# An output projection placed inside the attention's last head, earlier query rows, and wider fills of the relative terms

## The reference

```python
x = x + attention(layernorm(x, eps=1e-6))      # 12 heads of 32 channels
t = tokens(x)                                  # 2304 x 384
t = t + moe(layernorm(t, eps=1e-5))            # 8 experts, 1536 wide, top 2

# attention, per head; Rh, Rw gathered from relative position tables
attn = softmax((q * 32 ** -0.5) @ k.T + rel_h[..., :, None] + rel_w[..., None, :])
out = concat(attn @ v) @ proj_w + proj_b
```

## Time and profile before

| | |
|---|---|
| three timed runs | 2270.21 us median, 2269.88 to 2273.95 |
| profiled execution | 2271.55 us, its span 2269.8 us |
| busy in the span | PE 2056.3, PEld 1801.0, DVE 1423.4, ACT 1481.7, POOL 919.2 us |
| relative terms, DVE's first to last fill | 132.7 to 216.5 us |
| attention, last operation of DVE | 1444.9 us |
| projection, DVE's first and last operation | 1454.5 and 1523.6 us |
| gates, DVE's first operation | 1524.0 us |
| experts, POOL's first gather | 1617.1 us |

### The profile page before, as it was taken

How to read it: one execution, slowest core, us unless ns; L and a number is a source line. 1 busy time by engine, 2 the same in 40 slices (tenths; PEclk the granted TensorE clock), 3 DMA queues, 4 the chain that set the end, 5 groups by cost and what they waited for, 6 DMA issues and landing times. The chain is left out here.

```text
span 2269.8 us, 34244 instructions
## 1 busy us (share of the span) xinstructions
PE 2056.3 (91%) x11132; PEld 1801.0 (79%) x11132; DVE 1423.4 (63%) x2321; ACT 1481.7 (65%) x2533; POOL 919.2 (40%) x621
## 2 busy tenths in 40 slices
PE   6965589999999999999999999674799999999997
PEld 6932278888888888888888888462688888989997
DVE  5665679898998998989899996377333443110000
ACT  3354078888888888888888889412355555555554
POOL 0061323333333333333333334480555666555553
PEclk9955689999999999999999999787699999999999
DMA  6699933665546455563565534422433443211111
GB/s 215 220 253 271 182 84 69 117 112 104 108 73 133 87 111 94 106 131 71 110 113 107 113 66 99 129 101 73 160 85 105 140 125 99 49 37 29 29 29 15
DMA packets 92822, 247.02 MB, mean 109 GB/s; under 512 B 10168, under 2 KB 44440, under 8 KB 88420
## 3 DMA queue, kind: packets, MB, share of 16 engines
q1 hardware_dynamic: 81024, 223.57, 40.9%
q0 software_dynamic: 10672, 20.46, 5.4%
q10 hardware_dynamic: 960, 0.80, 0.1%
HBM read 179.27 MB, written 65.52 MB: 108 GB/s over the span
## 5 line engine op out<-in xcount | busy, mean ns | idle before, releaser
L896 DVE TENSOR_REDUCE mx<-ps_m 128x1 f32<-128x384 f32 x1212 | 643.7, 553 | 109.6 <-PE ps_m L751 104.3
L608 POOL TENSOR_TENSOR p_lo<-p_f,p_hi 128x768 fp32r<-128x768 f32 x216 | 398.1, 1843 | 767.8 <-ACT p_f L855 767.8
L849 ACT ACTIVATE p_hi<-ps_s 128x768 fp32r<-128x768 f32 x648 | 528.5, 816 | 147.2 <-PE ps_s L765 143.6
L855 ACT ACTIVATE p_f<-ps_s 128x768 f32<-128x768 f32 x648 | 525.7, 811 | 0.0
L751 PE MATMUL ps_m<-key_hi,query_hi 128*128 128x384 f32 x1240 | 419.4, 345 | 44.5 <-DMA query_hi<-rel_hi_d 35.7
L608 DVE TENSOR_TENSOR p_lo<-p_f,p_hi 128x768 fp32r<-128x768 f32 x432 | 414.2, 959 | 37.5 <-ACT p_f L855 36.4
L762 PE MATMUL ps_s<-query_hi,key_hi 128*128 128x384 f32 x1296 | 338.2, 342 | 10.4 <-DMA query_rest<-m_d 8.3
L775 PE MATMUL ps_o<-p_hi,val 128*65 128x384 f32 x1296 | 331.3, 337 | 1.7 <-POOL p_lo L608 1.7
L765 PE MATMUL ps_s<-query_rest,key_rest 121*128 121x384 f32 x1296 | 331.8, 337 | 0.0
L775 PE MATMUL ps_o<-p_lo,val 128*65 128x384 f32 x1296 | 331.5, 337 | 0.0
L751 PEld LDWEIGHTS ps_m<-key_hi,query_hi 128*128 128x128 f32 x1240 | 232.5, 189 | 89.0 <-DMA query_hi<-rel_hi_d 39.3
(11 more groups left out here) (247 smaller groups left out, 2242.5 us busy)
## 6 DMA issues: line engine op xcount, KB each, us to landing
query_rest<-rel_lo_d SPq DMA_DIRECT2D x36, 864.0 KB
query_rest<-qk_lo_d SPq DMA_DIRECT2D x36, 576.0 KB
query_rest<-qk_hi_d SPq DMA_DIRECT2D x36, 576.0 KB
query_hi<-rel_hi_d SPq DMA_DIRECT2D x12, 864.0 KB, 19.3
w_raw__19867<-w_u SPq DMA_DIRECT2D x12, 768.0 KB, 5.8
w_raw__19868<-w_u SPq DMA_DIRECT2D x12, 768.0 KB, 4.3
w_raw__19869<-w_u SPq DMA_DIRECT2D x12, 768.0 KB, 4.5
w_raw__19870<-w_u SPq DMA_DIRECT2D x12, 768.0 KB, 4.4
```

Source lines behind the costliest of these rows:

```text
L608: engine.tensor_tensor(p_lo[r][:], p_f[idx % 2], p_hi[r][:].bitcast(F32), ALU.subtract).then_inc(lo_done(0, idx)[0], 1)
L849: act.activation(p_hi[r][:], ps_s[:, bank:bank + 2, 0:TB], ACT.Exp).then_inc(hi_ok, 1)
L855: act.activation(p_f[idx % 2], ps_s[:, bank:bank + 2, 0:TB], ACT.Exp).then_inc(f_ok, 1)
L896: dve.tensor_reduce(mx[s // TILES][:, s // 3 % 6, col:col + 1], ps_m[:, c, 0:TB], AX.X, ALU.max).then_inc(mx_ok, 1)
```

## The change

**Projection into the last head.** `phase_proj` is gone. Its work stands in the attention stage. The heads 0 to 10 are projected for 18 tiles of 128 tokens by "all" jobs of nine matmuls; the last head is projected from ps_o's own copy by "own" jobs of three matmuls, and scaled afterwards, on the way out, by the reciprocal of its own sum, which a further column of the weights (C + 2 columns) carries along. Jobs stand on PE between the scores and `pv` of a unit, use the two halves of ps_m in turn, and are given units by two formulas: all t in unit 27 + 4t//3; own t < 6 in 29 + t, own 6 to 11 in 37 + t, own 12 to 17 after the loop. The proj_w rows are loaded at the end of head 8's list on SP (five DMAs) and split by POOL in units 11 and 14 of head 10 and by DVE in units 1 and 2 of the last head. The bias is a row of the weights against a row of ones.

The sums of heads 0 to 7 are loaded in head 10, those of 8 to 10 in the last head; DVE takes reciprocals (unit 26 of head 10; unit 12 of the last head), SP writes them and loads them back spread over 32 rows a head (`spread`, into `share`, the place of head 10's keys and queries, 8 and 3 DMAs of 288 KB). The spread of heads 0 to 7 stands in SP's list ahead of `load_max(11, 2)`. DVE multiplies in nine `scale` steps of 128x768 in units 11 to 16 and 21 to 23; POOL copies the high part of each tile, DVE subtracts for the low part two units before the job, and DVE evicts a job in the unit after it, with the bn_stats of the layernorm. x is loaded into the place of `share` as the scales free it. The last head's output is no longer stored to o_d.

**Query and key rows.** For h < 10, `load_hi(h + 2)` stands before the store of block 2 and waits for the scores of head h only.

**Wide fills.** CPB goes from 2 to 4: a fill is four matmuls in two PSUM banks (four rings of 4 x 256), 24 fills a group.

**Expert weights.** Expert 0's six pieces are no longer split in the projection. SP loads four of them at the start of the gates stage and two more ahead of the stores of blocks 2 and 3; POOL splits pieces 0 and 1 in the gates stage, DVE pieces 2 to 5 at the start of the experts stage, ahead of expert 1's.

```diff
 # phase_rel
-        CPB = 2
-        BANKS = 8
+        CPB = 4
+        RINGS = 4
+        WIDE = 256
-                        last = pe.matmul(ps[0:SIDE, bank, n * NQ:(n + 1) * NQ],
+                        last = pe.matmul(ps[0:SIDE, ring, n, 0:NQ],
...
 # phase_attention, SP
             def rest(h, par):
                 sp.wait_ge(pv_ok, UNITS * h + RING)
                 load_kv(h + 1, 1 - par)
                 for b in range(QBLOCKS):
+                    if b == QBLOCKS - 1 and h < HEADS - 2:
+                        sp.wait_ge(s_ok, UNITS * (h + 1))
+                        load_hi(h + 2, par)
                     store(h, par, b)
+                    if h == HEADS - 2 and b == 0:
+                        joins(QBLOCKS * EARLY)
+                        sp.dma_start(flat_early[:], flat(sums_d, 0, EARLY)).then_inc(sums_in, 16)
                     sp.wait_ge(s_ok, UNITS * h + TILES * (b + 1))
                     load_rest(h + 1, b)
+                    if h == HEADS - 2 and b == 0:
+                        for c in range(2):
+                            sp.dma_start(room[:, c, :], o_d[c * P:(c + 1) * P, :]).then_inc(early_in, 16)
+                    if h == HEADS - 2 and b == 1:
+                        sp.wait_ge(rec_ok, 1)
+                        sp.dma_start(flat(rec_d, 0, EARLY), flat_early[:]).then_inc(rec_out, 16)
                     if b < 2:
                         load_max(h + 1, b)
-                if h < HEADS - 2:
-                    sp.wait_ge(s_ok, UNITS * (h + 1) + LEAD)
-                    load_hi(h + 2, par)
+                if h == HEADS - 2:
+                    sp.wait_ge(s_ok, UNITS * (h + 1))
+                    sp.wait_ge(rec_out, 16)
+                    for c in range(2):
+                        spread(c, HPT)
+                    joins(QBLOCKS * (HEADS - 1))
+                    sp.dma_start(flat_late[:], flat(sums_d, EARLY, LATE)).then_inc(sums_in, 16)
+                    sp.wait_ge(raw_zero, 5)
+                    sp.dma_start(room[0:P - HD, 2, :], o_d[2 * P:C - HD, :]).then_inc(late_in, 16)
+                    sp.wait_ge(rec_ok, 2)
+                    sp.dma_start(flat(rec_d, EARLY, LATE), flat_late[:]).then_inc(rec_out, 16)
+                    sp.wait_ge(rec_out, 32)
+                    spread(2, LATE)
                 load_max(h + 1, 2)
+                if h == HEADS - 4:
+                    load_weights()
+                if h == HEADS - 2:
+                    for g in range(QBLOCKS):
+                        load_x(g)
...
 # phase_attention, PE
+            def tail(kind, t):
+                n = number_of[kind, t]
...
+                if n >= 2:
+                    pe.wait_ge(evicted, n - 1)
...
+                if kind == "all":
+                    pe.wait_ge(low_ok, t + 1)
+                    hi, lo = part_hi[t % len(part_hi)], lows[:, :, t * P:(t + 1) * P]
+                    for m, (v, w) in enumerate([(hi, w_hi), (hi, w_lo), (lo, w_hi)]):
+                        for k in range(KC):
+                            last = pe.matmul(ps_m[:, n % 2, 0:C], v[:, k, :], w[:, k, :], start=(m + k == 0), stop=(m == 2 and k == KC - 1))
+                else:
+                    b, c, cut = t // TPQ, t % TPQ // TPB, slice(t % TPB * P, (t % TPB + 1) * P)
+                    pe.wait_ge(acc_d, ACC + 2 * b + c + 1)
+                    for m, (v, w) in enumerate([(ot_hi, own_w_hi), (ot_hi, own_w_lo), (ot_lo, own_w_hi)]):
+                        last = pe.matmul(ps_m[:, n % 2, 0:C + 2], v[:, c, cut], w[:], start=(m == 0), stop=(m == 2))
+                last.then_inc(tail_mm, 1)
...
 # phase_attention, DVE
+            def scale(n):
+                c, cols = n // QBLOCKS, slice(n % QBLOCKS * QB, (n % QBLOCKS + 1) * QB)
+                rows = P if c < 2 else P - HD
+                if n == 0:
+                    dve.wait_ge(early_in, 32)
+                if n == 6:
+                    dve.wait_ge(late_in, 16)
+                if n % QBLOCKS == 0:
+                    dve.wait_ge(spread_in[c], 16 * (HPT if c < 2 else LATE))
+                dve.tensor_tensor(room[0:rows, c, cols], room[0:rows, c, cols], share[0:rows, c, cols], ALU.mult).then_inc(scaled, 1)
...
+            def added(kind, t):
+                n = number_of[kind, t]
...
+                    dve.reciprocal(rec[:, t:t + 1], ps_m[:, n % 2, C:C + 1]).then_inc(rec_made, 1)
+                    dve.wait_ge(evicted, n)
+                    dve.wait_ge(rec_made, t + 1)
+                    dve.scalar_tensor_tensor(x1[:, t, :], ps_m[:, n % 2, 0:C], rec[:, t:t + 1], x1[:, t, :], ALU.mult, ALU.add).then_inc(evicted, 1)
+                    if t > 0:
+                        measured(t - 1)
...
 # phase_gates, SP
-            for i in range(PIECES, PIECES + RAWS):
+            for i in range(RAWS):
                 moe.load_piece(sp, i)
...
+                if 2 <= blk < 2 + SPLIT_EARLY:
+                    sp.wait_ge(moe.w_ok, blk - 1)
+                    moe.load_piece(sp, RAWS + blk - 2)
                 sp.wait_ge(xn_ok, blk + 1)
```

More of the change, by code:

```diff
@@ L584, in phase_attention @@
         low_out = [sem(f"low_out{i}") for i in range(2)]
-        all_in = sem("all_in")
+        raw_zero = sem("raw_zero")
+        raw_in = sem("raw_in")
+        w_split = sem("w_split")
+        w_low = sem("w_low")
+        sums_in = sem("sums_in")
+        rec_ok = sem("rec_ok")
+        rec_out = sem("rec_out")
+        early_in = sem("early_in")
+        late_in = sem("late_in")
+        spread_in = [sem(f"spread_in{c}") for c in range(KC)]
+        scaled = sem("scaled")
+        x_in = [sem(f"x_in2_{b}") for b in range(QBLOCKS)]
+        part_ok = sem("part_ok")
+        low_ok = sem("low_ok")
+        tail_mm = sem("tail_mm")
+        evicted = sem("evicted")
+        rec_made = sem("rec_made")
         block = ctx.enter_context(nc.Block())
         loop_heads = OALL_HEADS
+        ACC = QBLOCKS * (HEADS - 1) + 1
+        TPQ = TILES // QBLOCKS
+        steps = {}
+        for t in range(TILES):
+            steps.setdefault(FIRST_TILE + 4 * t // 3, []).append(("all", t))
+            steps.setdefault((29 + t if t < TPQ else 37 + t) if t < 2 * TPQ else UNITS, []).append(("own", t))
+        order = [s for k in sorted(steps) for s in sorted(steps[k])]
+        number_of = {s: n for n, s in enumerate(order)}
+        unit_of = {s: k for k in steps for s in steps[k]}
         def chunk_at(h, par, k):
@@ L733, in head @@
                     n = QBLOCKS * h + idx // TILES - 1
-                    if idx % TILES == JOIN and idx < UNITS and n >= 0:
+                    if idx % TILES == JOIN and idx < UNITS and 0 <= n < QBLOCKS * (HEADS - 1):
                         joined(n)
+                    if h == HEADS - 2:
+                        if idx in SPLITS_AT:
+                            split_weights(SPLITS_AT.index(idx))
+                    if last:
+                        for t in range(TILES):
+                            if idx <= unit_of["all", t] - 2 < idx + POOL_EVERY:
+                                high_part(t)
             for idx in range(POOL_EVERY - 1, FIRST - 1, POOL_EVERY):
@@ L804, in head @@
                         half(tp, s, 0, ps_m)
+                    if last:
+                        for job in order:
+                            if unit_of[job] == k:
+                                tail(*job)
                     if k % TILES == 0:
-                        pe.wait_ge(acc_a, QBLOCKS * h + k // TILES + 1)
-                        pe.wait_ge(acc_d, QBLOCKS * h + k // TILES + 1)
+                        made = QBLOCKS * h + (k // TILES if not last else 2 * (k // TILES)) + 1
+                        pe.wait_ge(acc_a, made)
+                        pe.wait_ge(acc_d, made)
                     if k % TILES < TILES - 1:
@@ L813, in head @@
                         half(tp, s, 1, ps_m)
+                if last:
+                    for job in order:
+                        if unit_of[job] == UNITS:
+                            tail(*job)
             pe.wait_ge(hi_in[0], 48)
@@ L924, in head @@
                         negated(number, s)
+                    if last:
+                        for job in order:
+                            if unit_of[job] == k + 2 and job[0] == "all":
+                                low_part(job[1])
+                        for job in order:
+                            if unit_of[job] == k - 1:
+                                added(*job)
+                if last:
+                    for job in order:
+                        if unit_of[job] >= UNITS - 1:
+                            added(*job)
+                    measured(TILES - 1)
             dve.sem_inc(acc_d, 1)
@@ L1359, in _ @@
             pool.tensor_tensor(b2_lo[:], b2_raw[:], b2_hi[:].bitcast(F32), ALU.subtract).then_inc(b2_lo_ok, 1)
+            for i in range(SPLIT_EARLY):
+                moe.split_piece(pool, i)
             for t in range(TILES):
@@ L1819, in _ @@
         def _(dve):
```

(2 more changed lines are left out.)

341 lines of the change are left out of this document (149 added, 192 removed).

## The result

The changed kernel takes 2244.69 us in the median (four runs, 2238.38 to 2245.71), the kernel before 2270.05 beside it: ratio 0.9877, 95% interval [0.9857, 0.9897]. A later comparison gave 0.9886 [0.9865, 0.9906]. The profiled run took 2243.93, its span is 2242.2, 27.6 less than before.

What follows compares the result with a forecast made beforehand. PE was taken to bound the full heads, while no engine filled the projection. The terms - 5.8 - 2.0 - 25.4 + 0.5 + 2.4 = - 30.3 us took 2271.55 to 2241.2, or 2240 against the median; range 2228 to 2256.

Steps and rivals of the forecast that it cites:

- the fourth: Rival: earlier loads and wide fills give nothing, as another wait takes their place; 7.8 us less gain, 2248; chance 0.10.
- Query and key rows: Attention heads: loading these rows earlier removes PE's whole wait for them, minus 5.8 us (bounds minus 9.0 and minus 3).
- Wide fills: Attention's start: twelve wide fills save DVE 4.8 us, later restarts cost up to 2.0; taken as minus 2.0.
- in between: Among the wide fills: where the DMA engines are full, an earlier fill gives nothing; part of taking minus 2.0 us.
- The projection: Last head and after: the 79.6 us stage goes, less 34.8 matmuls, 8.5 DVE work, 10.9 after the loop: 25.4 us less.
- weight lows: Last head, units 1 and 2: DVE's low parts of the projection weights hold up its work by 1.5 us.
- the job units: Last head, units 27 to 49: 198 matmuls add 34.8 us on PE, nine units with both job kinds 2.2 more.
- rival 3: DVE and POOL block each other on SBUF operands: nine scales grow by 10.8 us, giving 2250; chance 0.12.
- Gates: Gates stage: two more loads ahead of stores, each after a POOL split ending in time; plus 0.5 us (0 to 6).
- Experts: Experts' start: expert 0's four splits on DVE slow two POOL subtractions on the filling pipeline's path; plus 2.4 us (0 to 6).
- Rival 2: Last head: spread sums arrive late, DVE waits in units 11, 12 or 21; 3 to 13 us, 2248; chance 0.12.
- Rival 1: Projection jobs: each waits for the eviction of the one just before; 40 us on top, 2280; chance 0.05.

Runs made afterwards that it cites:

- before_hi: The kernel before with only the next head's query and key rows loaded earlier, ahead of the store and of query_rest: 2261.16 us, ratio 0.9956.
- gate_late: The changed kernel with POOL's two early weight splits waiting until DVE has normalised all blocks, their reloads behind all stores of xn_d: 2243.61 us, ratio 0.9874.
- all_moved: The changed kernel with first m_d ahead of query_rest blocks 1 and 2, late POOL splits, weights' low parts in units 19 and 20, scales from unit 12: 2238.28 us.
- after_again: The changed kernel run again, nothing changed, on the chip of the follow-up runs as their base: 2246.58 us.

## Why the prediction was right

The forecast was 2240 us, the median is 2244.69; the mechanism held. Of the rivals, the half of the fourth that speaks of the wide fills came, and the third's mechanism at under a third of its price. By its terms, each from edges of the two traces (sum -27.6):

- *Query and key rows*, predicted -5.8, measured -5.2 by the maxima. That has the reciprocal in head 10 in it, which the prediction counts with the projection: over units 26 to 28 of that head PE's matmuls into ps_o fall back 0.8 us against before, as predicted. Without it the rows gave -6.0. The nearness hides two errors. The move alone is worth 8.3 (run before_hi), near the -9.0 of PE's weight loads that I kept as a bound; and the changed buffer addresses, which I put at nothing, cost 0.25 us a head, 2.3 over the heads in this count.

```profile
1307.07 1.04 DVE L1127 RECIPROCAL flat_early<-flat_early 128x144 f32<-128x144 f32 x1
```

- *Wide fills*, predicted -2.0, measured -0.4 at PE's first scores, within what these vary from run to run. DVE's sum was right (12 fills in 10.46 us against 24 in 11.24, and 2.3 to 2.9 with the queue out of the way). The step that failed is "in between": I let an earlier end count wherever the DMA engines weren't full among the fills, and didn't ask what stands after them, 4320 KB ahead of m_d.

```profile
134.77 10.46 DVE L528 TENSOR_TENSOR out_both<-ps,out_both 48x768 fp32r<-48x768 f32 x12 [6.93 <-ACT out_both L515]
```

- *The projection*, predicted -25.4, measured -23.7, or -22.9 with the reciprocal in head 10. One pair of traces doesn't give this to the us: from the end of the last but one block of maxima to the gates it takes 171.2 us in the trace of before and 168.1 to 170.3 in the three others with the old stage, 146.8 to 148.0 in eight with the change, 22.4 less between the means. The parts of the 23.7, by PE's starts of unit after unit against before: weight lows 1.4 (1.5); unit 11 with the step that follows 1.6 (0.8); units 12 to 16 2.2 (1.6); unit 18 1.0 (1.0); units 21 to 23 1.1 (0.6); the job units 37.6 (34.8 + 2.2); after the loop 11.1 (10.9). What was too small are the scales: nine take 11.6 us, where 0.95 each had been assumed, since those that start inside a POOL subtraction wait it out (3.45 for two at 1388.80, beside POOL's at 1388.07). That is rival 3's mechanism at 3.1 us on DVE, not 10.8: only some of the nine meet one. The Trainium skill, "SBUF — State Buffer", section "Who interferes with whom", says that the second to start waits for the whole of the first; g_lo's 3.42 beside 3.43 agrees, and so does its 0.17 without.
- *Gates*, predicted +0.5, measured +2.05 (3.2 between the means of the eight traces and the four). I had costed the two added loads and asked whether the splits end in time for the stores; I had not asked what DVE does while POOL splits. gate_late shows that this was the larger part.
- *Experts*, predicted +2.4, measured -0.3. It stays open: the time from the first gather to the end is 652.3 to 656.6 us in ten traces with the change and 652.6 to 655.1 in four without, so a term of 2 us can't be read from one pair. In this pair the first h_lo on POOL is as fast as before (1.26) and one of the next took 1.85.
- *Rival 2* stood closer than its chance of 0.12 said: DVE's waits for the loaded sums are 0.8 us in this trace, 0.4 to 2.1 in nine traces with the change, and 4.1 in all_moved, where DVE came sooner. In after_again, with 2.1, the last maxima come 1.3 us later against the block before them than here. *Rival 1*: 1.8 us of such waits, 6.7 once PE had less to do.

## What to carry to other kernels

Before a stage's gain is counted, follow the queue to the next thing that PE waits for: here 2.3 us on DVE vanished ahead of a 3 KB transfer, and letting that transfer go first was worth 11 us, two fifths of what the whole change brought. A term that comes out right should be run alone, since its size may be two errors that cancel. And work moved out of a full engine's way can uncover the transfer that it used to hide.

## What the runs showed of the hardware that was not expected

- With the second query and key buffers at other addresses, and without any wait on a DMA, a head takes 96.45 us in the changed kernel, 96.20 in before_hi. The difference arises in units 12 to 53, where scores and maxima read different buffers (0.17 to 0.27 us), and not up to unit 11, where both read the same (0.00 to 0.05). In the one run of the kernel before with only the addresses changed, head 0 shows the same, and the loads land after 19.9 instead of 19.1 to 19.4 us.
- A DVE tensor_scalar with one array from SBUF is held up by POOL's splits too: six xnn took 4.51 us beside them, 3.11 without.
